# First attention of a linear-attention and expert kernel: keys also made with tokens on the partitions, their maximum taken off by TensorE, residual and b_out written into z's banks by VectorE

## The reference

```python
def attn(x, gamma, beta, w_qkv, w_out, b_out):        # 4 heads of 32
    xn = layernorm(x) * gamma + beta
    q, k, v = split(xn @ w_qkv); q = q * 32 ** -0.5
    k = softmax(k, axis=tokens)
    context = einsum('bnhd,bnhe->bhde', k, v)
    out = einsum('bhde,bnhd->bnhe', context, q) @ w_out + b_out
    return out + x
def ffn(x, Wg, Wu, Wd):                               # 8 experts, 512 wide
    return sum((silu(x @ Wg[e]) * (x @ Wu[e])) @ Wd[e] for e in range(8))
x = x + layernorm(attn(layernorm(x), ...))
x = x + layernorm(ffn(layernorm(x), ...))
```

## Time and profile before

| what | us |
|---|---|
| median of the runs (lowest to highest of 3) | 552.12 (551.99 to 552.26) |
| profiled execution | 552.13 |
| its span | 550.3 |
| TensorE busy in the span | 541.6 (98%) |
| VectorE busy | 439.3 (80%) |
| ScalarE busy | 347.4 (63%) |
| GpSimd busy | 160.5 (29%) |

### The profile page before, as it was taken

One profiled execution on the slowest core, in us unless ns is written; L12 is line 12 of the kernel. 1 busy time (PEld: TensorE's weight loads), 2 busy tenths in 40 slices (PEclk: granted clock), 3 DMA queues, 4 the chain that ended last, 5 costly groups with the idle time before them and its releaser, 6 DMA issues.

```text
span 550.3 us, 8696 instructions
## 1 busy us (share of the span) xinstructions
PE 541.6 (98%) x2642; PEld 466.8 (85%) x2643; DVE 439.3 (80%) x978; ACT 347.4 (63%) x626; POOL 160.5 (29%) x205
## 2 busy tenths in 40 slices
...
DMA packets 29329, 25.47 MB, mean 46 GB/s; under 512 B 3169, under 2 KB 21986, under 8 KB 29282
## 3 DMA queue, kind: packets, MB, share of 16 engines
q1 hardware_dynamic: 27984, 24.19, 13.9%
...
...
## 4 chain that ended last, share of the span: by engine, by line
PE 95%; ACT 2%; DVE 2%; issue 1%; POOLq 0%; DVEq 0%; POOL 0%; ACTq 0%
PE gate_ps L1073 10%; PE acc_ps L1076 10%; PE acc_ps L1074 10%; PE acc_ps L1073 10%; PE gate_ps L1074 10%; PE up_ps L1074 10%; PE up_ps L1076 10%; PE gate_ps L1076 10%; PE up_ps L1073 10%; PE att_ps L1131 1%; PE att_ps L1119 1%; PE up_ps L1177 1%; ACT h_hi L636 1%; PE att_ps L1107 1%; ACT gs L659 1%
## 5 line engine op out<-in xcount | busy, mean ns | idle before, releaser
L659 ACT ACTIVATE gs<-gate_ps 128x512 f32<-128x512 f32 x255 | 152.0, 596 | 175.1 <-PE gate_ps L1076 172.2
L883 DVE TENSOR_TENSOR h<-gs,up_ps 128x512 f32<-128x512 f32 x234 | 159.8, 683 | 89.9 <-PE up_ps L1076 84.8
L870 DVE TENSOR_TENSOR h_lo<-h,h_hi 128x512 fp32r<-128x512 f32 x234 | 173.2, 740 | 0.1
L636 ACT ACTIVATE h_hi<-h 128x512 fp32r<-128x512 f32 x234 | 145.8, 623 | 7.5 <-DVE h L883 6.9
L1073 PE MATMUL gate_ps<-x1nT_hi,wg_hi 128*128 128x512 f32 (+1 forms) x254 | 98.5, 388 | 0.0
L1076 PE MATMUL acc_ps<-h_lo,wd_hi 128*128 128x512 f32 x254 | 96.5, 380 | 1.7 <-DVE h_lo L870 1.6
L1073 PE MATMUL acc_ps<-h_hi,wd_hi 128*128 128x512 f32 x254 | 96.3, 379 | 0.3 <-ACT h_hi L636 0.3
L1073 PE MATMUL up_ps<-x1nT_hi,wu_hi 128*128 128x512 f32 (+1 forms) x254 | 96.2, 379 | 0.2 <-POOL wu_lo L346 0.2
L1074 PE MATMUL acc_ps<-h_hi,wd_lo 128*128 128x512 f32 x254 | 96.3, 379 | 0.0
L1076 PE MATMUL gate_ps<-x1nT_lo,wg_hi 128*128 128x512 f32 (+1 forms) x254 | 96.1, 378 | 0.0
L1074 PE MATMUL up_ps<-x1nT_hi,wu_lo 128*128 128x512 f32 (+1 forms) x254 | 96.1, 378 | 0.0
...
## 6 DMA issues: line engine op xcount, KB each, us to landing
...
t_out_x1n<-t_dram_x1n SPq DMA_DIRECT2D x28, 64.0 KB, 2.0
...
t_out_acc<-t_dram_acc SPq DMA_DIRECT2D x28, 64.0 KB, 2.0
```

What stands on the lines that cost most here:

```text
L636: act.activation(h_hi[s % NH][:, :], h_of(t, s)[:, :], ACT.Copy).then_inc(s_hhi, 1)
L659: act.activation(gs[q][:, :], gate_ps[q][:, :], ACT.Silu).then_inc(s_silu, 1)
L870: dve.tensor_tensor(h_lo[s % NH][:, :], h_of(t, s)[:, :], h_hi[s % NH][:, :].bitcast(F32), ALU.subtract).then_inc(s_hlo, 1)
L883: dve.tensor_tensor(h_of(t, s)[:, :], gs[q][:, :], up_ps[q][:, :], ALU.mult).then_inc(s_h, 1)
```

## The change

In the first attention:

- The keys are made twice: with features on the partitions, as before, but into two banks, and with tokens on the partitions (`first_k`). The maximum is taken in two halves and combined. ScalarE writes its negative on a diagonal (`kmax_diag`), and a TensorE product of ones with that diagonal adds it to each key bank (`first_k_less_max`). ScalarE's exponential of these banks is `Ek`. The transposes of `ET` and the copies behind them are gone. `ET` itself is made later, in one instruction that also gives the sum.
- b_out is added by VectorE together with the residual (`first_yb`): it writes both into z's bank, and TensorE adds q M to that. The TensorE products `output_bias` and `residual` and ScalarE's `residual` are gone. One product of ones with b_out on a zeroed 128 x 128 tile makes b_out on all partitions.
- The load of w_qkv is cut in two, b_out's load moves from ScalarE's queue to SP's, behind a wait for the zeroed tile.
- TensorE makes U before it transposes x; `wqT`, `bm`, `R_sb` and `U_sb` are made by ScalarE at other places, U in two halves.
- Batch 1's `xh` is made by ScalarE instead of GpSimd. GpSimd makes small terms for batches 1 and 2 (`scales_of_input`) that VectorE made, and `next_scale` replaces one power by two. VectorE's `x_stats` in the first body ends with the averages.
- Fillers: 7, 2, 2, 1, 2 at five places (start, behind z, behind batch 1's transposes, behind its keys, behind the first x1n) instead of 8, 5, 2, 6, 2 (start, behind w's transposes, then the same last three). `LO_AFTER` loses block 7.
- `split_hi` of blocks 3 and 4 and the `next_residual` calls stand at other places of ScalarE's order.

The diff, cut to its core; removed lines are mostly left out, since the kernel above shows them. First the tables, SP, GpSimd and ScalarE:

```diff
-BUSY = {"start": 8, "w": 5, "xn": 2, "attn": 6, "x1n": 2}
+BUSY = {"start": 7, "z": 2, "xn": 2, "attn": 1, "x1n": 2}
...
-LO_AFTER = {5: 1, 6: 3, 7: 5}
+LO_AFTER = {5: 1, 6: 3}
...
-            sp.dma_start(wqkv[:, :], w_qkv).then_inc(s_wqkv, 16)
+            sp.dma_start(wqkv[:, 2 * D:3 * D], w_qkv[:, 2 * D:3 * D]).then_inc(s_wv, 16)
+            sp.dma_start(wqkv[:, 0:2 * D], w_qkv[:, 0:2 * D]).then_inc(s_wqk, 16)
             sp.dma_start(wout[:, :], w_out).then_inc(s_wout, 16)
+            sp.wait_ge(s_bout_zero, 1)
+            sp.dma_start(bout[0:1, :], b_out.rearrange("(a d) -> a d", a=1)).then_inc(s_bout, 16)
...
+            def scales_of_input(c):
+                pool.wait_ge(s_mv["x"], c)
+                if c == 1:
+                    pool.wait_ge(s_f_r0, 1)
+                else:
+                    pool.wait_ge(s_f_next_nmr, 2)
+                pool.tensor_scalar(ve["x"][:, 1, :], mv["x"][:, :, 1], 1.0 + EPS, EPS * EPS, ALU.mult,
+                                   ALU.add).then_inc(s_ve["x"], 1)
+                pool.tensor_scalar(ve["x"][:, 0, :], mv["x"][:, :, 1], EPS, None, ALU.add).then_inc(s_ve["x"], 1)
+                pool.tensor_scalar(nm["x"][:, :], mv["x"][:, :, 0], -1.0, None, ALU.mult).then_inc(s_nm["x"], 1)
...
+                    if c == 2:
+                        scales_of_input(c)
                     power("x", c * 2, 2, s_rstd["x"])
...
+            pool.wait_ge(s_f_kmax, 1)
             split_lo(pool, 0)
...
+            def next_scale(which):
+                pool.wait_ge(s_ve["x"], 2)
+                pool.wait_ge(s_nm["x"], 1)
+                pool.tensor_tensor(rstd["x"][:, which, :], ve["x"][:, which, :], expo[:, 0:J],
+                                   ALU.pow).then_inc(s_f_next_r, 1)
+                pool.wait_ge(s_f_next_r, 2 - which)
+                last = pool.tensor_tensor(next_nmr[:, which, :], nm["x"][:, :], rstd["x"][:, which, :], ALU.mult)
+                last.then_inc(s_f_next_nmr, 1)
+            scales_of_input(1)
+            next_scale(1)
             split_lo(pool, 1)
...
             half_power("x1", 1, rstd["x1"])
+            next_scale(0)
+            pool.sem_inc(s_rstd["x"], 1)
...
+            act.wait_ge(s_bv_ps, 1)
+            act.activation(bv[:, :], up_ps[2][:, 2 * D:2 * D + 1], ACT.Copy).then_inc(s_bv, 1)
+            act.wait_ge(s_bv, 1)
+            act.wait_ge(s_mask, 2)
+            act.activation(bm[:, :], head_mask[:, :], ACT.Copy, scale=bv[:, 0:1]).then_inc(s_bm, 1)
+            def scaled_U(i):
+                heads = slice(i * HEADS // 2, (i + 1) * HEADS // 2)
+                return act.activation(U_sb[:, heads, :], gate_ps[2][:, i * 2 * D:(i + 1) * 2 * D], ACT.Copy,
...
             act.wait_ge(s_gb, 32)
...
+            act.wait_ge(s_f_xT, 1)
+            act.activation(xnT[:, HALF], gate_ps[0][:, HALF], ACT.Identity, bias=bcol[:, 0:1],
+                           scale=gcol[:, 0:1]).then_inc(s_f_xnT, 1)
+            act.wait_ge(s_R_ps, 1)
+            act.activation(R_sb[:, :], up_ps[2][:, 0:D], ACT.Copy).then_inc(s_R, 1)
+            act.wait_ge(s_U_ps, 1)
+            scaled_U(0)
             split_hi(0)
             split_hi(1)
             act.wait_ge(s_f_kmax, 1)
...
+            act.activation(kmax_diag[:, :], ident[:, :], ACT.Copy, scale=kmax_neg[:, 0:1]).then_inc(s_f_kdiag, 1)
+            for i, ps in enumerate((gate_ps[0][:, HALF], up_ps[0][:, REST])):
+                act.wait_ge(s_f_k, i + 1)
+                act.activation(Ek[:, i * JH:i * JH + JH, :], ps, ACT.Exp).then_inc(s_f_E, 1)
+            scaled_U(1).then_inc(s_U, 1)
+            act.wait_ge(s_wq_ps, 1)
+            act.activation(wqT[:, :], up_ps[1][:, 0:D], ACT.Copy, scale=Q_SCALE).then_inc(s_wqT, 1)
+            act.activation(two(ET[:, :]), key_ps, ACT.Exp, bias=kmax_neg[:, 0:1], scale=1.0,
+                           accum_out=esum[:, 0:1]).then_inc(s_f_esum, 1)
             act.wait_ge(s_f_qT_ps, 1)
...
+            act.activation(qT_v[:, HALF], up_ps[0][:, HALF], ACT.Copy, scale=Q_SCALE).then_inc(s_f_qT, 1)
+            def next_xh(j):
+                return act.activation(xh[:, j, :], x_in[1][:, j, :], ACT.Identity, bias=next_nmr[:, 1, j:j + 1],
+                                      scale=rstd["x"][:, 1, j:j + 1])
+            def next_residual(j):
+                return act.activation(yb[:, j, :], x_in[1][:, j, :], ACT.Identity, bias=next_nmr[:, 0, j:j + 1],
+                                      scale=rstd["x"][:, 0, j:j + 1])
+            act.wait_ge(s_f_A_ps, 1)
+            act.wait_ge(s_f_next_nmr, 1)
+            next_xh(0)
             act.wait_ge(s_f_qT_ps, 2)
...
+            act.activation(qT_v[:, REST], att_ps[:, REST], ACT.Copy, scale=Q_SCALE).then_inc(s_f_qT, 1)
...
+            for j in range(1, J):
+                last = next_xh(j)
+            last.then_inc(s_xh, 1)
             split_hi(2)
...
+            act.wait_ge(s_f_yb, J)
...
+            split_hi(3)
...
+            split_hi(4)
             split_hi(5)
...
+            act.wait_ge(s_f_next_nmr, 2)
+            next_residual(0)
             act.wait_ge(s_f_n, 2)
             act.activation(blocks_of(x1nT_hi[0][:, :], 1), two(acc_ps[:, REST]), ACT.Copy).then_inc(s_x1nT_hi, 1)
+            for j in range(1, J):
+                last = next_residual(j)
+            last.then_inc(s_y, 1)
```

VectorE:

```diff
+                    if first:
+                        token_stats("x", x_in[par])
+                        means_and_variances("x", c)
+                    else:
+                        stats_of("x", c, x_in[par], n_ve=2)
+                        negative_mean("x")
...
             dve.wait_ge(s_xa, 16)
             first_stats("x", 0, x_in[0][:, 0, :])
             first_stats("x", 1, x_in[0][:, 1, :])
+            first_aggregate("x", 0)
+            first_variance("x", 0, 1)
             dve.wait_ge(s_xb, 16)
             first_stats("x", 2, x_in[0][:, 2, :])
...
             dve.wait_ge(s_gb, 32)
...
+            dve.wait_ge(s_f_xT, 2)
+            dve.tensor_scalar(xnT[:, REST], up_ps[0][:, HALF], gcol[:, 0:1], bcol[:, 0:1], ALU.mult,
+                              ALU.add).then_inc(s_f_xnT2, 1)
+            for i, ps in enumerate((acc_ps, att_ps)):
+                dve.wait_ge(s_f_kT, i + 1)
+                dve.tensor_reduce(kmax_half[:, i:i + 1], ps[:, HALF], AX_X, ALU.max,
+                                  negate=True).then_inc(s_f_kmax_half, 1)
+            dve.wait_ge(s_f_kmax_half, 2)
+            dve.tensor_reduce(kmax_neg[:, 0:1], kmax_half[:, :], AX_X, ALU.min).then_inc(s_f_kmax, 1)
...
+            def first_yb(j):
+                dve.scalar_tensor_tensor(out=z_ps[j], in0=x_in[0][:, j, :], scalar=first_rstd[:, 0, j:j + 1],
+                                         in1=up_ps[2][:, D:2 * D], op0=ALU.mult, op1=ALU.add).then_inc(s_f_yb, 1)
             dve.wait_ge(s_f_r0, 1)
...
+            dve.wait_ge(s_bout_ps, 1)
+            dve.wait_ge(s_wvT, HEADS)
+            first_yb(0)
+            dve.wait_ge(s_wqT, 1)
+            first_yb(1)
             dve.wait_ge(s_f_A_ps, 1)
...
+            dve.tensor_copy(A_sb[:, :], gate_ps[0][:, 0:D]).then_inc(s_f_A, 1)
+            dve.wait_ge(s_U, 1)
+            first_yb(2)
             dve.wait_ge(s_f_esum, 1)
             dve.reciprocal(erec[:, :], esum[:, :]).then_inc(s_f_erec, 1)
             dve.wait_ge(s_f_erec, 1)
             dve.wait_ge(s_R, 1)
...
+            dve.scalar_tensor_tensor(out=M_sb[:, :], in0=gate_ps[0][:, D:2 * D], scalar=erec[:, 0:1], in1=R_sb[:, :],
                                      op0=ALU.mult, op1=ALU.add).then_inc(s_f_M, 1)
+            first_yb(3)
```

TensorE:

```diff
+                pe.wait_ge(s_f_yb, j + 1)
                 pe.wait_ge(s_f_qT, j // JH + 1)
-                pe.matmul(tile_banks[j][:, 0:D], qT_v[:, j * P:j * P + P], M_sb[:, :], start=False,
-                          stop=True).then_inc(s_f_z, 1)
+                pe.matmul(z_ps[j], qT_v[:, j * P:j * P + P], M_sb[:, :], start=False, stop=True,
+                          skip_group_check=True).then_inc(s_f_z, 1)
...
+            pe.wait_ge(s_wv, 16)
             pe.transpose(gate_ps[1][:, 0:D], wqkv[:, 2 * D:3 * D], ident[:, :]).then_inc(s_w_ps, 1)
...
+            pe.wait_ge(s_wqk, 16)
+            pe.transpose(up_ps[1][:, 0:D], wqkv[:, 0:D], ident[:, :]).then_inc(s_wq_ps, 1)
+            pe.wait_ge(s_gb, 32)
+            pe.matmul(up_ps[2][:, 2 * D:2 * D + 1], wqkv[:, 2 * D:3 * D], bcol[:, 0:1], start=True,
+                      stop=True).then_inc(s_bv_ps, 1)
+            pe.wait_ge(s_wout, 16)
+            for hd in range(HEADS):
+                pe.wait_ge(s_wvT, hd + 1)
+                last = pe.matmul(gate_ps[2][:, hd * D:hd * D + D], wvT_bd[:, hd, :], wout[:, :], start=(hd == 0), stop=(hd == HEADS - 1))
+            last.then_inc(s_U_ps, 1)
...
+            def first_kT(i, half):
+                pe.matmul((acc_ps, att_ps)[i][:, HALF], wqkv[:, D:2 * D], xnT[:, half], start=True,
+                          stop=True).then_inc(s_f_kT, 1)
```

(31 more changed lines are left out.)

187 lines of the change are left out of this document (38 added, 149 removed).

## The result

| what | before | after |
|---|---|---|
| median of 5 runs (lowest to highest), us | 552.12 (551.85 to 552.59) | 548.85 (548.74 to 550.46) |
| ratio to before, 95% interval | | 0.9946 (0.9932 to 0.9961) |
| profiled execution, us | 552.13 | 550.46 |
| its span, us | 550.3 | 548.7 |
| start of the first full gate product, us | 25.31 | 25.90 |

The profiled execution is the longest of the five, by 1.35 us over the next. Its 18 executions fall into two heaps: nine of 548.74 to 549.53 us and nine of 550.46 to 551.19 us. On the first chip four of five were short ones, on the others five of 13. So "548.85" is a short execution's time. The changed kernel has to be read in both kinds.

What follows compares the result with a forecast made beforehand. TensorE, busy 98%, was taken to bound the kernel, with gains possible only in the first attention and the first batch's steps. 0.9 - 0.6 + 0.2 + 0.1 - 1.8 - 0.3 = -1.5 from 552.1 gave 550.6 us, range 549.3 to 552.3.

Steps and rivals of the forecast that it cites:

- the sum for the first attention: First attention up to M: M starts at 14.5 us against 13.61, 0.9 us late.
- the term for U: Start of first attention: w_out lands at 6.0 us, U ends at 7.0, transposes start at 7.1 instead of 6.69.
- hand-over: From first attention to expert steps: `next_residual(0)` waits for GpSimd, second half of x1nT_hi starts 0.2 us late.
- z's gain: First attention after M: all four z products run at once, VectorE goes on without a pause, 0.6 us gained.
- TensorE's wait for h's high part grows: After the hand-over: first SiLU is later, TensorE's wait of 0.3 us for ScalarE grows by 0.1 us.
- first batch's steps: First batch's expert steps, up to 46 us: TensorE's waits for VectorE and GpSimd go, 1.8 and 0.3 us gained.
- third rival: First attention: the early U is hidden, w_out lands by 5.3 us; 550.0 us, or 549.7 with a free handover; chance 0.18.
- second rival: First attention: TensorE's clock rises some us later, 1.0 us late, 551.6 us; chance 0.18.
- fifth rival: TensorE's clock stays at 1.2 GHz through the first attention, 5.0 us added, 555.6 us; chance 0.06.
- the trio: First batch's steps: three small VectorE instructions for batch 2 go to GpSimd, 1.8 us gained.
- block 7: First batch's steps: GpSimd makes weight block 7's low part at 31.3 us, TensorE's 0.23 us wait goes, 0.3 us gained.
- fourth rival: First batch's steps: GpSimd subtractions beside low parts of h put back 1.5 of 1.8 us, 552.1 us; chance 0.08.

Runs made afterwards that it cites:

- after_fifth: The changed kernel, unchanged, run again for one profiled execution, with the clock's rise at 5.4 us; 549.03 us.
- after_fillers: The changed kernel with eight leading fillers and two behind b_v's product; 549.63 us, on a second chip 549.95 us.
- after_again: The changed kernel, unchanged, run again on another chip; median 550.65 us (549.53 to 551.10).
- after_third: The changed kernel, unchanged, run again, with the clock's rise at 5.3 us in its profile; median 550.00 us (548.80 to 551.19).
- after_fourth: The changed kernel, unchanged, run again for one profiled execution, with the clock's rise at 9.5 us; 550.77 us.
- late_U: after_fillers with TensorE's U products moved, heads 0 and 1 behind the k products, heads 2 and 3 behind the maximum's products; 549.62 us.

## Why the prediction missed

**The step that failed** is the sum for the first attention, +0.9 for M and +0.5 with z and the hand-over, and in it above all the term for U: w_out landing at 6.0 us, U ending at 7.0 and the transposes starting at 7.1, where they started at 6.32. In its own terms, against `after_fifth`, the execution with the clock up as the forecast took it:

| term | forecast | measured | off by |
|---|---|---|---|
| transposes of x-hat start | 7.1 | 6.32 | 0.78 |
| from there to the first key product | 1.2 | 1.09 | 0.11 |
| key product to maximum | 2.0 | 2.00 | 0 |
| maximum to A | 3.0 | 2.83 | 0.17 |
| A to M | 1.2 | 1.06 | 0.14 |
| z's gain (M to x1, 3.46 before) | 0.6 | 0.77 | 0.17 |
| hand-over, x1 to gate product | 0.2 | 0.23 | -0.03 |
| TensorE's wait for h's high part grows | 0.1 | 0 | 0.1 |
| first batch's steps | 2.1 | 2.26 | 0.16 |
| sum | -1.5 | -3.1 | 1.6 |

Half of the miss is one term: U's place. I had w_out land at 6.0 us from the 4.0 us to landing of the earlier trace rows. In the changed kernel the same 64 KB land 2.7 and 2.8 us after their issue in the two executions shown, TensorE starts U at 5.3 straight behind b_v's product, and U is out of the way by 6.3. VectorE makes x-hat's four tiles from 5.46 to 6.77 us, so U holds the first two back by some 0.2 us at most (an estimate from these rows). That is the third rival's mechanism, which had 0.18; its times, 550.0 and 549.7, carried the other errors too. `after_fillers` is the control: with U at 6.04 the transposes start at 6.93 and the gate product 0.61 us later. The other half is six terms, each 0.10 to 0.17 us too dear, and one, the hand-over, 0.03 too cheap: durations added with rounded waits between them. The range, 1.3 us below the forecast, had no room for that.

The long executions, 550.5 to 551.2 us, and the median of `after_again`, 550.65, lie at or near the forecast of 550.6. That would have been luck: in them the late clock costs about what the sum had too dear.

**Clock.** The second rival was real, and mis-sized and mis-weighted. It was given 0.18, 1.0 us and 551.6. Nine of 18 executions lie in its heap, three of them profiled; there the gate product starts 1.4 to 1.7 us later than in `after_fifth` (1.1 to 1.4 than in `after_third`). The times are still only 550.5 to 550.8, since everything else was cheaper than taken. Between the two executions shown, U costs 0.82 us, the way to the first key product 0.26 and that from there to the maximum 0.37; the rival had counted 0.9, 0.2 and 0.2, less what waits for x anyway. A median over such a kernel depends on how many executions of each kind the sample holds; on the first chip it was four short of five. The fifth rival didn't occur.

**First batch's steps.** The size was right, 2.1 forecast and 2.25 to 2.26 measured, and so were the rows to look at. The account wasn't: 1.8 for the trio and 0.3 for block 7 are not two independent gains. Each edit takes the same collision away, and block 7's alone is worth 2.35. The sentence "GpSimd reaches that place with a shorter queue" named the right fact and drew only a bound from it. The fourth rival, GpSimd's subtractions beside each low part of h, cost nothing that the profile shows: those low parts take 1.1 to 1.2 us before and after.

**Hand-over.** Right in size (0.2 forecast, 0.23 measured from x1 to the gate product: 25.90 - 17.43 = 8.47 against 8.24), although undoing the wait gained nothing.

No version that I ran is shorter than the changed kernel's short executions. The plainest, the kernel before with block 7's entry deleted, comes to 549.86 us with its five executions within 0.7 us; on the same chip the whole change gave 550.00, from 548.80 to 551.19.

**Open.** What decides in an execution whether the clock rises at 5 or at 9 us. In 15 of the 20 profiles of all versions it first rises between 3.9 and 6.3 us, in five between 9.3 and 9.6, in none between. `after_third` and `after_fourth` do the same work up to 5.1 us, with the same wait for w_qk (0.55 and 0.56 us), and the clock rises at 5.3 in one and at 9.5 in the other; so neither the number of fillers nor that gap settles it, though the ten executions with two fillers hold no long one. Not settled either is how much of the first attention's gain would be left without the early U: the one profile of `late_U` has the late clock.
